# Value projection four heads at a time, and another order of work between the first attention and the expert blocks

## The chip, the cores and the metric

The kernel runs on one core of a Trainium2 chip. The time is device microseconds of one execution; the time before is the median of three runs. The profile is of a further execution of the same program. Engines are named as in the profile: PE (TensorE, with PEld for its weight loads), DVE (VectorE), ACT (ScalarE), POOL (GpSimd), SP (SyncE, which here only issues DMAs).

## The reference

Four sublayers, each `x = x + layernorm(f(layernorm(x)))`, on 2 x 1024 tokens of 128 features in float32. The change touches the first attention and the start of the first feed-forward:

```python
# first attention: 16 heads of 64
qkv = (X @ W_qkv).reshape(b, s, 16, 64, 3); q, k, v = qkv[..., 0], qkv[..., 1], qkv[..., 2]
weights = softmax(einsum('bqhd,bkhd->bhqk', q, k) / 8)
attn = einsum('bhqk,bkhd->bqhd', weights, v); return attn.reshape(b, s, 1024) @ W_out
# first feed-forward: one shared expert and the best 2 of 8 experts, all 128 -> 512 -> 128
normed = hidden * rsqrt(mean(hidden ** 2) + 1e-8) * norm_weight
shared = relu(normed @ sw1 + sb1) @ sw2 + sb2
probs = sigmoid(flat @ router_w.T); scores, idx = top_k(probs, 2)
w = scores / (sum(scores) + 1e-6)     # eo: each expert's output
return shared + sum over the two experts of w * eo
```

The second attention (8 heads, differential) and the gated feed-forward behind it are as before in both kernels.

## The kernel before, in words

Each engine has its own program, written out by hand in order; semaphores tie them together. A value in float32 is held as a rounded part ("hi") and a remainder ("lo"), both in the type fp32r, and a product is two or three matmuls.

**First attention (a0).** 16 heads, one after another. A head has 16 slots, one for each tile of 128 queries (8 tiles of batch 0, then 8 of batch 1). In a slot PE makes the scores (4 matmuls of 512 columns, L643, L644), then perhaps one extra piece, then the 8 transposes of the weights of three slots ago (L611), then 4 matmuls of weights by values (L621, L622). DVE takes the row maximum (L785), its share of the extra piece, and the lo parts of the transposed weights (L771, two of 512). ACT makes exp (L750) and the hi parts (L720). POOL divides by the row sum (L844, L848). The scores have two buffers, the transposed weights two half banks.

The extra pieces are in the table `A0_PIECES`, indexed by the head's place in its pair: `qk` projects queries and keys of a later stretch (3 matmuls of 512), `v` projects values, `out` adds the output projection (8 matmuls of 128). All go through one PSUM bank, `ps_m`: a piece waits until DVE has read the one before (`a0_bank_free`). A `v` piece is 512 tokens by the 128 columns of two heads: per 128 tokens three matmuls of 128 columns (L585 to L587); ACT copies the bank as the hi part (L691), DVE subtracts (L704). `a0_pairs` runs the first pair of heads, a hardware loop of six pairs, and the last pair.

SP places queries and keys with four small DMAs per `qk` piece (`a0_place_qk`), each set behind the previous one. Early in head 0 it also issues the nine loads of the expert weights w1 (`f0_load_early`, 256 KB each), and in head 1 the clearing of the row buffers in DRAM (`f0_clear_rows`).

**Tail and first feed-forward (f0).** The 2048 tokens are 4 chunks of 512. For each, DVE does the norm of the attention's output, adds it to X and norms again in five stages (`y0_norm(stage, chunk)`: 0 statistics of Y, 1 apply, 2 add, 3 statistics of X, 4 apply), with the reciprocal root from POOL (`norm_rstd`, `norm_rstd_rms`). Then PE turns the chunk (`f0_pe_turn`), ACT copies it twice, DVE makes its lo part (`f0_dve_turn`), PE makes router logits (`f0_pe_logits`) and the shared expert (`up`, `down`). For each half of the tokens DVE ranks the experts (`f0_dve_route`: 17 small dependent operations), PE sums prefixes (`route`), DVE works out positions (`f0_dve_place`), and POOL scatters the rows with indirect DMAs (L1475, 16 for a half). Meanwhile w1 is split: ACT copies each of nine pieces as hi (`f0_act_w1_hi`, L982), POOL subtracts (`f0_pool_w1_lo`, L986). When both halves are placed, PE, ACT and DVE read the experts' numbers (`f0_read_words`) and the 46 expert blocks start.

## Time and profile before

| what | value |
|---|---|
| median of 3 runs | 2009.54 us (2009.08 to 2011.68) |
| the profiled execution | 1990.03 us |
| its span, first to last instruction | 1988.2 us |
| granted TensorE clock, mean | 0.971 |
| PE / DVE / ACT / POOL busy | 92% / 78% / 68% / 60% |

The first attention ends at about 875 us, the stretch to the first expert block at about 943 us. A row of the timeline gives start and duration in us, and in brackets how long the engine sat idle before it and what ended that. A matmul's duration is its way through the array; matmuls overlap, so what one costs PE is the distance from its start to the next one's. Where a line groups instructions, the mean is of one.

### The profile page before, as it was taken

The page shows a single profiled execution, that of the slowest core. Times are in us where ns is not written, and L with a number is a line of the kernel's source. Part 1 is how long each engine was busy: PE and PEld are TensorE (multiplying, and loading weights), DVE is VectorE, ACT ScalarE, POOL GpSimd, SP SyncE. Part 2 cuts the span into 40 slices and gives each one's busy share as a digit, 9 for nine tenths or more (in the row PEclk, how much of TensorE's full clock was granted, in tenths as well). Part 3 has the DMA queues.
Part 4 walks back from the last instruction along what each step waited for, and adds up shares of the span by engine and source line. Part 5 has one row for each costly group of instructions (what it writes and reads, how often), then busy time and mean ns, then how long its engine had stood idle before and what let it go on. Part 6 is the DMA issues. An engine that isn't in the chain of part 4 may idle for free.

```text
span 1988.2 us, 37557 instructions
## 1 busy us (share of the span) xinstructions
PE 1838.5 (92%) x11354; PEld 1569.9 (79%) x11354; DVE 1558.7 (78%) x2650; ACT 1351.4 (68%) x2707; POOL 1195.9 (60%) x1481
## 2 busy tenths in 40 slices
PE   4959999999999999985986899999999999999787
PEld 3858888888888888864875688888888888888666
DVE  5958989898989898975577777777777777777775
ACT  3847878787878787841554577777777777777555
POOL 4534646565656465645655577777777777778621
PEclk8979999999999999997998899999999999999899
DMA  4291212121212121112211000000000000100000
GB/s 117 52 82 47 46 40 51 40 51 34 53 35 53 33 55 36 42 49 81 75 58 33 3 1 12 1 11 0 11 0 11 0 11 0 66 1 1 1 11 12
DMA packets 68473, 65.25 MB, mean 33 GB/s; under 512 B 27713, under 2 KB 47041, under 8 KB 68129
## 3 DMA queue, kind: packets, MB, share of 16 engines
q1 hardware_dynamic: 65888, 59.02, 13.7%
q0 software_dynamic: 2496, 5.15, 0.7%
q8 instruction: 44, 0.72, 0.2%
q14 instruction: 45, 0.36, 0.1%
HBM read 21.33 MB, written 9.25 MB: 15 GB/s over the span
## 4 chain that ended last, share of the span: by engine, by line
PE 41%; DVE 7%; issue 4%; ACT 2%; POOL 1%; DVEq 0%; ACTq 0%; POOLq 0%
PE ps_s L1804 5%; PE ps_s L1803 5%; PE ps_s L1805 5%; PE ps_t L1861 3%; PE ps_o L1877 3%; PE ps_o L1879 3%; PE ps_o L1878 3%; PE ps_t L1290 2%; DVE a_negmax L2007 2%; PE ps_m L1898 1%; PE ps_t L1585 1%; PE ps_s L2239 1%; PE ps_s L2240 1%; PE ps_m L1900 1%; PE ps_m L1899 1%
## 5 line engine op out<-in xcount | busy, mean ns | idle before, releaser
L785 DVE TENSOR_REDUCE a_negmax<-ps_s 128x1 f32<-128x1024 f32 x256 | 313.4, 1224 | 73.8 <-PE ps_s L644 59.3
L2007 DVE TENSOR_REDUCE a_negmax<-ps_s 128x1 f32<-128x1024 f32 x256 | 312.3, 1220 | 67.5 <-PE ps_s L1805 64.8
L720 ACT ACTIVATE a_pth<-ps_t 128x512 fp32r<-128x512 f32 x512 | 278.6, 600 | 113.5 <-PE ps_t L611 113.4
L1935 ACT ACTIVATE a_p<-ps_s,a_negmax 128x1024 f32<-128x1024 f32 x256 | 286.4, 1119 | 95.3 <-DVE a_negmax L2007 94.1
L844 POOL TENSOR_TENSOR a_rsum<-a_sum,minus_one 128x1 f32<-128x1 f32 x256 | 141.1, 551 | 329.3 <-ACT a_p L750 328.0
L771 DVE TENSOR_TENSOR a_ptl<-ps_t,a_pth 128x512 fp32r<-128x512 f32 x512 | 327.5, 681 | 6.6 <-ACT a_pth L720 5.8
L848 POOL TENSOR_SCALAR a_p<-a_p,a_rsum 128x1024 f32<-128x1024 f32 x256 | 289.0, 1129 | 52.9 <-POOL a_rsum L844 52.9
L2105 POOL TENSOR_TENSOR a_p<-a_p 128x1024 f32<-128x1024 f32 x128 | 307.4, 2401 | 10.7
L750 ACT ACTIVATE a_p<-ps_s,a_negmax 128x1024 f32<-128x1024 f32 x256 | 288.5, 1127 | 15.3 <-DVE a_negmax L785 15.3
L643 PE MATMUL ps_s<-a_kh,a_q 128*128 128x512 f32 x512 | 202.5, 395 | 30.3 <-DMA a_kl<-a_kl 19.8
L611 PEld LDWEIGHTS ps_t<-ident_r,a_pr 128*128 128x128 f32 x2048 | 200.7, 141 | 31.9 <-POOL a_p L848 4.0
L621 PE MATMUL ps_o<-a_pth,a_v 128*128 128x512 f32 x512 | 220.3, 430 | 3.6 <-ACT a_o L729 2.0
L611 PE MATMUL ps_t<-ident_r,a_pr 128*128 128x128 f32 x2048 | 210.1, 246 | 3.5 <-DVE a_ptl L771 3.5
L1803 PE MATMUL ps_s<-xT_hi,a_q 128*128 128x512 f32 x512 | 203.6, 398 | 7.0 <-ACT a_p L1935 7.0
L1959 ACT ACTIVATE a_ath<-ps_t 128x512 fp32r<-128x512 f32 x256 | 139.2, 596 | 99.2 <-PE ps_t L1861 98.4
L1804 PE MATMUL ps_s<-xT_lo,a_q 128*128 128x512 f32 x512 | 203.0, 397 | 0.0
L1805 PE MATMUL ps_s<-xT_hi,a_q 128*128 128x512 f32 x512 | 202.7, 396 | 0.0
L644 PE MATMUL ps_s<-a_kl,a_q 128*128 128x512 f32 x512 | 202.3, 395 | 0.0
L622 PE MATMUL ps_o<-a_ptl,a_v 128*128 128x512 f32 x512 | 202.0, 395 | 0.0
L2043 DVE TENSOR_TENSOR a_atl<-ps_t,a_ath 128x512 fp32r<-128x512 f32 x256 | 163.6, 680 | 0.5 <-ACT a_ath L1959 0.5
L2099 POOL TENSOR_SCALAR a_p<-a_p,a_c 128x1024 f32<-128x1024 f32 x128 | 144.4, 1128 | 21.9 <-DVE a_c L2020 20.0
L1877 PE MATMUL ps_o<-a_ath,a_xh 128*128 128x256 f32 x512 | 148.2, 289 | 0.6 <-DVE a_atl L2043 0.6
(299 smaller groups left out, 4220.8 us busy)
## 6 DMA issues: line engine op xcount, KB each, us to landing
a_q<-a_kh SPq DMA_DIRECT2D x64, 128.0 KB, 2.2
a_q<-a_kl SPq DMA_DIRECT2D x64, 128.0 KB, 2.4
a_kh<-a_kh SPq DMA_DIRECT2D x64, 128.0 KB, 2.2
a_kl<-a_kl SPq DMA_DIRECT2D x64, 128.0 KB, 2.3
a_w_raw<-in_l_w SPq DMA_DIRECT2D x8, 384.0 KB
f_xs_rows<-f_zero SPq DMA_DIRECT2D x4, 736.0 KB, 20.3
f_raw<-in_ffn_w SPq DMA_DIRECT2D x2, 1408.0 KB, 7.5
f_xs<-f_xs_rows SPq DMA_DIRECT2D x2, 1235.0 KB
```

The lines of the kernel that those rows point to most:

```text
L611: ins = pe.transpose(ps_t[:, half, j * P:(j + 1) * P].bitcast(F32R), a0_pr[q % 4][:, k0:k0 + P], ident_r[:, :])
L720: act.activation(a0_pth[(q // 4) % 2][a0_pt_part(q, half)], ps_t[:, half, :].rearrange("p (t c) -> p t c", c=P), ACT.Copy)\
L750: act.activation(a0_p[s % 4][:, :], ps_s[:, s % 2, :, :], ACT.Exp, bias=a0_negmax[:, s % 4:s % 4 + 1], accum_out=a0_sum[:, s % 4:s % 4 + 1 ...
L771: dve.tensor_tensor(a0_ptl[(q // 4) % 2][at], ps_t[:, half, :].rearrange("p (t c) -> p t c", c=P), a0_pth[(q // 4) % 2][at], ALU.subtract) ...
L785: dve.tensor_reduce(a0_negmax[:, s % 4:s % 4 + 1], ps_s[:, s % 2, :, :], AX.XY, ALU.max, negate=True)\
L848: pool.tensor_scalar(a0_p[s % 4][:, :], a0_p[s % 4][:, :], a0_rsum[:, s % 4:s % 4 + 1], 1.0, ALU.mult, ALU.mult).then_inc(S["a0_p_normed"], 1)
L1803: pe.matmul(dst, a1_q[b][m][:, 0, qs], xT_hi[:, k], start=True, stop=False)
L1804: pe.matmul(dst, a1_q[b][m][:, 0, qs], xT_lo[:, k], start=False, stop=False)
L1805: ins = pe.matmul(dst, a1_q[b][m][:, 1, qs], xT_hi[:, k], start=False, stop=True)
L1935: act.activation(a1_p[s % 4][m][:, :], ps_s[:, m, :, :], ACT.Exp, bias=a1_negmax[:, s % 2, m:m + 1], accum_out=a1_sum[:, s % RING, m:m + 1 ...
L2007: dve.tensor_reduce(a1_negmax[:, s % 2, m:m + 1], ps_s[:, m, :, :], AX.XY, ALU.max, negate=True)\
L2105: pool.tensor_tensor(p1, p1, p2, ALU.add).then_inc(S["a1_combined"], 1)
```

## The change

1. The heads go in fours (`QUAD`, `a0_quads`: first four, a loop of two fours, last four). A `v` piece is now 256 tokens by the 256 columns of four heads: six matmuls of 256 columns in place of twelve of 128. There are eight in the first head of a four and none in the third; each is split by two ACT copies and two DVE subtractions of 256 in place of one each of 512. In all there are 32 `v` pieces before and after.
2. The values' buffer is laid out anew and reaches into the place of w1's raw copy, so w1 is loaded in head 14, when the products of head 13 are done.
3. In the attention's tail: stages of chunk 0's norm go behind the last row maximum; chunk 1's stages 0 to 3 go ahead of DVE's lo part of chunk 0; all nine hi parts of w1 go on ACT ahead of chunk 0's copies, and POOL's nine lo parts follow.
4. Behind the first `up`: chunk 1 is turned and both logits are made, then `down(0)` (with the route's prefix sums inside), `up(1)`, `down(1)`. ACT's relu comes behind the probabilities.

```diff
-            {0: ("out", 1), 1: ("qk", 1, 0), 2: ("v", 0, 0), 3: ("qk", 1, 1), 4: ("out", 2), 5: ("v", 0, 1), 8: ("out", 3),
-             9: ("v", 1, 0), 10: ("qk", 0, 0), 12: ("qk", 0, 1), 13: ("v", 1, 1)},
+            {0: ("out", 1), 1: ("qk", 1, 0), 2: ("v", 0, 0), 3: ("qk", 1, 1), 4: ("out", 2), 5: ("v", 0, 1), 6: ("v", 0, 2),
+             7: ("v", 0, 3), 8: ("out", 3), 9: ("v", 1, 0), 10: ("qk", 0, 0), 11: ("v", 1, 1), 12: ("qk", 0, 1),
+             13: ("v", 1, 2), 14: ("v", 1, 3)},
...
+        def a0_v_of(j, b):
+
+            return a0_v[:, 1 - j // 2, b, :, j % 2, :]
...
+        def a0_quads(eng, body):
+
+            def quad(p, first, last):
+                for j in range(QUAD):
+                    body(p, j, p * QUAD + j, first and j == 0, last and j == QUAD - 1)
+
+            heads(eng, H0 // QUAD, quad)
...
-                for i in range(TPC):
-                    x = slice(b * SEQ + half * BANK + i * P, b * SEQ + half * BANK + (i + 1) * P)
-                    dst = ps_m[:, i * P:(i + 1) * P]
+                for i in range(2):
+                    x = slice(b * SEQ + (2 * half + i) * P, b * SEQ + (2 * half + i + 1) * P)
+                    dst = ps_m[:, i * QUAD * DH0:(i + 1) * QUAD * DH0]
...
-                        if s in (A0_LAG_PV, A0_LAG_PV + KT):
-                            pe.wait_ge(S["a0_split_lo"], a0_splits(p, j, s - 1, last))
+                        if j == 0 and A0_LAG_PV <= s < A0_LAG_PV + 4 or j == 0 and s == A0_LAG_PV + KT:
+                            pe.wait_ge(S["a0_split_lo"], a0_splits(p, j, s - 2, last))
...
-                ins = act.activation(a0_v[b][:, half * TPC:(half + 1) * TPC, :, 0:DH0], src, ACT.Copy)
+                for w in range(2):
+                    ins = act.activation(a0_v[:, w, b, 2 * half:2 * half + 2, :, 0:DH0], src[:, w, :, :, :], ACT.Copy)
...
-                ins = dve.tensor_tensor(v[:, :, :, DH0:2 * DH0], src, v[:, :, :, 0:DH0], ALU.subtract)
+                for w in range(2):
+                    v = a0_v[:, w, b, 2 * half:2 * half + 2, :, :]
+                    ins = dve.tensor_tensor(v[:, :, :, DH0:2 * DH0], src[:, w, :, :, :], v[:, :, :, 0:DH0], ALU.subtract)
...
+            sp.wait_ge(S["a0_pv"], 4 * (H0 - 2))
             for e in range(NE):
                 sp.dma_start(f0_w1_raw[:, e, :], t["ffn0_w1"][:, e, :]).then_inc(S["f0_w1_loaded"], 16)
...
+                    if isinstance(p, int) and p == H0 // QUAD - 1 and j == QUAD - 2 and i == 1:
+                        f0_load_early(sp)
...
             up(0)
+            f0_pe_turn(pe, 1)
             pe.wait_ge(S["a0_out_added"], 2 * H0)
             f0_pe_logits(pe, 0)
-            down(0)
-            f0_pe_turn(pe, 1)
             f0_pe_logits(pe, 1)
+            down(0, lambda: route(0))
             up(1)
-            down(1, lambda: route(0))
+            down(1)
```

**The values on PE.** PE's rows in slot 2 of the first head, from the scores to the next slot's scores. Before (the start of a piece of twelve):

```order
L644 MATMUL ps_s<-a0_kl0,a0_q0 128x512
L585 MATMUL ps_m<-a0_wv_hi,xT_hi 128x128 [waits a0_wv_lo,a0_split_lo]
L586 MATMUL ps_m<-a0_wv_lo,xT_hi 128x128
L587 MATMUL ps_m<-a0_wv_hi,xT_lo 128x128
L585 MATMUL ps_m<-a0_wv_hi,xT_hi 128x128
L586 MATMUL ps_m<-a0_wv_lo,xT_hi 128x128
L587 MATMUL ps_m<-a0_wv_hi,xT_lo 128x128
L585 MATMUL ps_m<-a0_wv_hi,xT_hi 128x128
```

After, the whole piece:

```order
L658 MATMUL ps_s<-a0_kl0,a0_q0 128x512
L599 MATMUL ps_m<-a0_wv_hi,xT_hi 128x256 [waits a0_wv_lo,a0_split_lo]
L600 MATMUL ps_m<-a0_wv_lo,xT_hi 128x256
L601 MATMUL ps_m<-a0_wv_hi,xT_lo 128x256
L599 MATMUL ps_m<-a0_wv_hi,xT_hi 128x256
L600 MATMUL ps_m<-a0_wv_lo,xT_hi 128x256
L601 MATMUL ps_m<-a0_wv_hi,xT_lo 128x256
L657 MATMUL ps_s<-a0_kh0,a0_q0 128x512 [waits a0_exped]
```

Twelve matmuls of 128 columns became six of 256.

**The norms on DVE.** DVE's rows around the last row maximum of the attention (`f0_staged0` is chunk 0's norm, `ptl` the lo parts). Before:

```order
L785 TENSOR_REDUCE a0_negmax<-ps_s 128x1 [waits a0_scores]
L771 TENSOR_TENSOR a0_ptl0<-ps_t,a0_pth0 128x4x128 [waits a0_pt_hi] x2
L371 TENSOR_SCALAR f0_staged0<-Y,mv,rstd 128x128 [waits norm_rstd]
L371 TENSOR_SCALAR f0_staged0<-Y,mv,rstd 128x128 x3
L785 TENSOR_REDUCE a0_negmax<-ps_s 128x1 [waits a0_scores]
L771 TENSOR_TENSOR a0_ptl1<-ps_t,a0_pth1 128x4x128 [waits a0_pt_hi] x2
L943 TENSOR_TENSOR X<-X,f0_staged0 128x512 [waits dve_step]
```

After:

```order
L807 TENSOR_REDUCE a0_negmax<-ps_s 128x1 [waits a0_scores]
L793 TENSOR_TENSOR a0_ptl0<-ps_t,a0_pth0 128x4x128 [waits a0_pt_hi] x2
L807 TENSOR_REDUCE a0_negmax<-ps_s 128x1 [waits a0_scores]
L793 TENSOR_TENSOR a0_ptl1<-ps_t,a0_pth1 128x4x128 [waits a0_pt_hi] x2
L373 TENSOR_SCALAR f0_staged0<-Y,mv,rstd 128x128 [waits norm_rstd]
L373 TENSOR_SCALAR f0_staged0<-Y,mv,rstd 128x128 x3
L793 TENSOR_TENSOR a0_ptl1<-ps_t,a0_pth1 128x4x128 [waits a0_pt_hi] x2
L976 TENSOR_TENSOR X<-X,f0_staged0 128x512 [waits dve_step]
```

The last row maximum and the lo part behind it passed the four apply operations.

**The tail on ACT.** ACT's rows from the first hi part of w1 on (`a0_o2` are the attention's last outputs, `f0_nT`, `xT_hi` the turned chunk, `f0_h` the shared expert's relu). Before:

```order
L729 ACTIVATE a0_o20<-ps_o 128x512 [waits a0_out_in,a0_pv]
L967 ACTIVATE f0_nT0<-ps_t,f0_nw 128x512 [waits f0_logits,x_turned,f0_small_loaded]
L460 ACTIVATE xT_hi<-ps_t,f0_nw 128x512 [waits x_turned]
L729 ACTIVATE a0_o21<-ps_o 128x512 [waits a0_out_in,a0_pv]
L982 ACTIVATE f0_w1_hi<-f0_w1_raw 128x512 [waits f0_w1_loaded]
L1335 ACTIVATE f0_h00<-ps_s,f0_b1 128x512 [waits f0_up]
```

After:

```order
L747 ACTIVATE a0_o20<-ps_o 128x512 [waits a0_out_in,a0_pv]
L1015 ACTIVATE f0_w1_hi<-f0_w1_raw 128x512 [waits f0_w1_loaded] x6
L747 ACTIVATE a0_o21<-ps_o 128x512 [waits a0_out_in,a0_pv]
L1000 ACTIVATE f0_nT0<-ps_t,f0_nw 128x512 [waits f0_logits,x_turned,f0_small_loaded]
L462 ACTIVATE xT_hi<-ps_t,f0_nw 128x512 [waits x_turned]
L1000 ACTIVATE f0_nT1<-ps_t,f0_nw 128x512 [waits f0_logits,x_turned]
L462 ACTIVATE xT_hi<-ps_t,f0_nw 128x512 [waits x_turned]
L1034 ACTIVATE f0_prob<-ps_m 128x64 [waits f0_logits]
L1368 ACTIVATE f0_h00<-ps_s,f0_b1 128x512 [waits f0_up]
```

Six hi parts stand between the last two outputs, and the first relu stands behind chunk 1's copies and the probabilities.

## Rows read from the trace of the kernel before

**Rows 1.** The page: busy time and share of the span, by engine.
```profile
PE 1838.5 (92%) x11354; PEld 1569.9 (79%) x11354; DVE 1558.7 (78%) x2650; ACT 1351.4 (68%) x2707; POOL 1195.9 (60%) x1481
```
**Rows 2.** Windows: stretch, its length, busy of each engine, PEclk, DMA share, GB/s.
```profile
460.00:560.00 100.00, 99.64 (x640) 85.83 (x640) 87.82 (x112) 79.20 (x147) 55.78 (x71) 1.00 0.18 43
```
**Rows 3.** Timeline of PE: a v piece's first matmul, and what follows its twelfth.
```profile
256.86 0.23 PE L585 MATMUL ps_m<-a_wv_hi,xT_hi 128*128 128x128 f32 x1
...
258.15 0.85 PE L611 MATMUL ps_t<-ident_r,a_pr 128*128 128x128 f32 x8
```
**Rows 4.** Timeline of PE: twelve matmuls of 256 columns in the second attention.
```profile
1302.05 0.28 PE L1877 MATMUL ps_o<-a_ath,a_xh 128*128 128x256 f32 x1
...
1303.47 0.39 PE L1803 MATMUL ps_s<-xT_hi,a_q 128*128 128x512 f32 x1
```
**Rows 5.** Timeline of DVE: row maxima that begin a qk, a plain and a v slot.
```profile
205.94 1.23 DVE L785 TENSOR_REDUCE a_negmax<-ps_s 128x1 f32<-128x1024 f32 x1
...
209.20 1.22 DVE L785 TENSOR_REDUCE a_negmax<-ps_s 128x1 f32<-128x1024 f32 x1
...
220.09 1.22 DVE L785 TENSOR_REDUCE a_negmax<-ps_s 128x1 f32<-128x1024 f32 x1
...
222.64 1.23 DVE L785 TENSOR_REDUCE a_negmax<-ps_s 128x1 f32<-128x1024 f32 x1
...
257.06 1.23 DVE L785 TENSOR_REDUCE a_negmax<-ps_s 128x1 f32<-128x1024 f32 x1
...
260.94 1.23 DVE L785 TENSOR_REDUCE a_negmax<-ps_s 128x1 f32<-128x1024 f32 x1
```
**Rows 6.** Lines by form: copies and subtractions from PSUM of 512 and of 256.
```profile
L691 ACT ACTIVATE a_v<-ps_m 128x512 fp32r<-128x512 f32 x32 | 19.2, 599 | 40.1 <-PE ps_m L587 40.1
L1968 ACT ACTIVATE a_zh<-ps_o 128x256 fp32r<-128x256 f32 x64 | 24.0, 375 | 2.1 <-PE ps_o L1879 2.1
L704 DVE TENSOR_TENSOR a_v<-ps_m,a_v 128x512 fp32r<-128x512 f32 x32 | 22.1, 692 | 22.1 <-ACT a_v L691 22.0
L2049 DVE TENSOR_TENSOR a_zl<-ps_o,a_zh 128x256 fp32r<-128x256 f32 x3 | 1.3, 422 | 1.8 <-ACT a_zh L1968 1.8
```
**Rows 7.** Timeline: PE's wait in the attention's tail, first up, chunk 1's turn.
```profile
855.75 1.25 PE L611 MATMUL ps_t<-ident_r,a_pr 128*128 128x128 f32 x8 [1.86 <-DVE a_ptl L771]
...
875.41 0.48 PE L1232 MATMUL ps_s<-xT_hi,f_w_hi 128*128 128x512 f32 x1
...
882.91 0.60 PE L454 MATMUL ps_t<-ident,f_staged 128*128 128x128 f32 x4
```
**Rows 8.** Timeline: POOL's lo parts of w1 over DVE's first route, one same operation later.
```profile
887.43 8.66 POOL L986 TENSOR_TENSOR f_w_lo<-f_w_raw,f_w_hi 128x512 fp32r<-128x512 f32 x7
...
891.32 1.19 DVE L1020 TENSOR_TENSOR f_tmp<-f_tmp,f_rank 128x64 f32<-128x64 f32 x1
...
899.86 0.17 DVE L1061 CAST f_pos<-f_place 128x16 int32<-128x16 f32 x1
...
928.03 0.22 DVE L1020 TENSOR_TENSOR f_tmp<-f_tmp,f_rank 128x64 f32<-128x64 f32 x1
```
**Rows 9.** Timeline of PE: chunk 2's turn, and the first turn of the expert blocks.
```profile
908.62 1.11 PE L454 MATMUL ps_o<-ident,f_staged 128*128 128x128 f32 x4 [7.70 <-DVE f_staged L371]
...
936.67 0.50 PE L1262 MATMUL ps_o<-ident_r,f_xs 128*128 128x128 f32 x4 [4.09 <-issue]
```
**Rows 10.** Timeline: four apply operations of DVE, undisturbed and while POOL works.
```profile
876.30 1.11 DVE L371 TENSOR_SCALAR f_staged<-Y,mv,rstd 128x128 f32<-128x128 f32 x4
...
1106.79 3.96 DVE L371 TENSOR_SCALAR xhat<-Y,mv,rstd 128x128 f32<-128x128 f32 x4
...
1108.21 2.46 POOL L2105 TENSOR_TENSOR a_p<-a_p 128x1024 f32<-128x1024 f32 x1
```
**Rows 11.** Timeline: PE's wait in head 2; DMA view: w1's loads, KB each, us to landing.
```profile
145.34 0.79 PE L643 MATMUL ps_s<-a_kh,a_q 128*128 128x512 f32 x1 [19.76 <-DMA a_kl<-a_kl]
...
f_w_raw<-in_ffn_w SPq DMA_DIRECT2D x9, 256.0 KB, 4.5
```

More of the change, by code:

```diff
@@ L80, in sandwich_kernel @@
         A0_END = 137 * KB
+        QUAD = 4
         A1_KEYS = 109 * KB
@@ L538, in sandwich_kernel, with a0_pair @@
         A0_SPLITS = [[s for s in pieces if pieces[s][0] != "out"] for pieces in A0_PIECES]
-        A0_PAIR_SPLITS = len(A0_SPLITS[0]) + len(A0_SPLITS[1])
+        A0_QUAD_SPLITS = sum(len(z) for z in A0_SPLITS)
+        def a0_pair(p, j):
+            return p * 2 + j // 2
         def a0_piece(j, s, first, last):
             piece = A0_PIECES[j].get(s)
-            if piece is None or (first and piece[0] == "out" and j == 0) or (last and j == 1 and s in A0_NEXT):
+            if piece is None or (first and piece[0] == "out" and j == 0) or (last and j == QUAD - 1 and s in A0_NEXT):
                 return None
@@ L548, in a0_splits @@
         def a0_splits(p, j, s, last):
-            n = sum(1 for z in A0_SPLITS[j] if z <= s and not (last and j == 1 and z in A0_NEXT))
-            return p * A0_PAIR_SPLITS + (len(A0_NEXT) + j * len(A0_SPLITS[0]) + n)
+            n = sum(1 for z in A0_SPLITS[j] if z <= s and not (last and j == QUAD - 1 and z in A0_NEXT))
+            return p * A0_QUAD_SPLITS + (len(A0_NEXT) + sum(len(z) for z in A0_SPLITS[:j]) + n)
         def a0_outs(p, j, s):
-            return p * 4 + (3 * j - 3 + sum(1 for z in A0_PIECES[j] if z <= s and A0_PIECES[j][z][0] == "out"))
+            return a0_pair(p, j) * 4 + (3 * (j % 2) - 3 + sum(1 for z in A0_PIECES[j] if z <= s and A0_PIECES[j][z][0] == "out"))
         def a0_bank_free(pe, p, j, s, first, last):
@@ L565, in a0_bank_free @@
                 pe.wait_ge(S["a0_split_lo"], a0_splits(p, j, z, last))
-        def a0_pairs(eng, body):
-            def pair(p, first, last):
-                for j in range(2):
-                    body(p, j, p * 2 + j, first and j == 0, last and j == 1)
-            heads(eng, H0 // 2, pair)
+        def a0_quads(eng, body):
[3 more added lines that the diff above has]
+            heads(eng, H0 // QUAD, quad)
         def first_bank(i):
@@ L907, in body @@
                     sp.dma_start(a0_wqk_raw[:, :], row(t["l0_wqk"], h + 1)).then_inc(S["a0_wqk_loaded"], 16)
-                if j == 1 and not last:
+                if j == QUAD - 1 and not last:
                     sp.wait_ge(S["a0_wv_lo"], p + 1)
```

120 lines of the change are left out of this document (63 added, 57 removed), and 3 rows, old and new, of the table A0_PIECES.

## The prediction

> **What bounds the kernel now.** I read the busy shares first, then windows, then timelines of the two places that the change touches. PE is busy for 92% of the span [rows 1]. In the steady part of the first attention it is busy for 99.64 of 100 us at the full granted clock, DVE for 87.82, ACT for 79.20, POOL for 55.78 [rows 2]: PE sets the pace there and every us taken from its queue counts, as long as DVE, the next one, stays below it. It is close in a plain slot: the row maxima of two plain slots stand 2.55 us apart (222.64 - 220.09), and DVE needs one maximum and two lo parts in it. A `qk` slot takes 3.26 us and a `v` slot 3.88 [rows 5]. Behind the attention nobody is full. From 875 to 943 us the time goes along a chain: chunk 1's norm, turn and logits, the route on DVE, positions, chunk 2's norm between POOL's scatters, its turn on PE at 908.62 after 7.70 us of idling, and at the end the reading of the experts' numbers before PE turns the first expert rows at 936.67 [rows 9].
>
> **The values, four heads a pass.** Twelve matmuls of 128 columns take PE from 256.86 to 258.15, 1.29 us or 0.108 each; a `v` slot is longer than a plain one by 3.88 - 2.55 = 1.33 us [rows 3, 5]. Twelve matmuls of 256 columns in the second attention go from 1302.05 to 1303.47, 1.42 us or 0.118 each, again in fp32r with a new weight tile for each [rows 4]. So a matmul of half the columns costs nearly as much, and six of 256 cost 6 x 0.118 = 0.71 us where twelve of 128 cost 1.29 to 1.33. There are 32 pieces before and 32 after. Saved on PE: 32 x 0.60 = 19.2 us.
>
> The Trainium skill (TensorE: Matmul & The Clock Gate, "Back-to-back issue gap") gives, for a matmul alone, 134 cycles for 128 columns and 262 for 256. By that twelve small ones cost what six large ones cost, and the merge gives nothing; the trace has 0.108 us for 128 columns, about twice that rule, and 0.118 for 256, so it disagrees for the small one, and I follow the trace. It stays a rival below.
>
> Against it stands the split. ACT's copy of 512 takes 599 ns, of 256 375, so two take 750: 0.15 us more. DVE's subtraction takes 692 and 422, two 844: 0.15 us more [rows 6]. They lie beside PE as long as DVE keeps up. A `qk` slot, built the same way, costs 3.26 - 2.55 = 0.71 us over a plain one [rows 5]; a `v` slot should be the same if DVE and ACT hide their part, and 0.30 more if neither does: 3.26 to 3.56 us, against 3.88. Ends: 32 x 0.60 = 19.2 and 32 x 0.32 = 10.2. I take 18.5, near the upper end, since the slots of 4 heads average out: only the first head of four holds `v` pieces, its `out` slots leave DVE idle, and DVE has 12 us of slack in 100 [rows 2]. The bank `ps_m` is now used in 15 of 16 slots there; before, slots 0 to 5 already followed each other without a PE wait.
>
> Waits added. PE's waits for `a0_split_lo` ask for pieces of two slots ago, which the bank's own wait has already asked for: 0. SP now waits in head 14 for the products of head 13 (slot 6) before the w1 loads, and behind it in its queue stand the two last placements of head 14, from slot 10 on, some 10 us later. Each load landed 4.5 us after its issue at the start of the kernel [rows 11]; if the nine hardly overlapped they would take 9 x 1 us and more, still within those 10, and head 15 needs the placements only at its start, nine slots of at least 2.55 us after slot 6: hidden. Taking the loads away from head 0 gains nothing: PE's 19.76 us wait in head 2 [rows 11] comes behind the clearing of the rows, which stays. Two more small value loads stand ahead of three of the X loads: +0.5 us, between 0 and 1. The loop is entered half as often; no wait stands at its branches, so 0.
>
> **The tail.** (a) The last row maximum no longer waits for the four apply operations, so the 1.86 us that PE waits at 855.75 go [rows 7]: -1.9. (b) POOL's seven lo parts of w1 lie over DVE's route, 887.43 to 896.09, and seven of its two-input operations take 0.94 to 1.21 us each in place of about 0.22 (1.19 against 0.22 for the same line later) [rows 8]: 7.7 us in place of 1.6. With w1 split ahead of it: -6.1. (c) Chunk 1's turn comes at 882.91, 7.5 us behind the start of the first `up` [rows 7], after logits, `down(0)` and a norm that started late. After the change the norm's stages 0 to 3 run while PE does the last output pieces, and the turn follows `up` at once: `up` is twelve matmuls of twice the columns of rows 4, 2 x 1.42 = 2.8 us, so up to 7.5 - 2.8 = 4.7 us are saved; and the first `up` itself starts 2 to 3 us sooner, since nothing of chunk 0 waits behind the last output: -7 together if nothing interferes. (d) Something does: POOL's nine lo parts now lie over chunk 0's last apply and chunk 1's stages 1, 2 and 4, ten DVE operations on SBUF. Rows of before show what happens to them: four apply operations that take 1.11 us undisturbed took 3.96 with POOL at work, ending with its 2.46 us operation [rows 10]. At one lo part each (8.66 / 7 = 1.24 us [rows 8]) in place of 0.26 the ten lose up to 9.8 us, partly in waits that are there anyway: +5, between 0 and 9.8. (e) PE idles for the relus, which now stand behind the probabilities, before `down(0)`: four of about the 0.6 us of rows 6, near 3 us with the handover; but the route runs beside it and is the longer way, and `up(1)`, `down(1)` end about when chunk 2 is ready for its turn: 0 to +3.
>
> The positions of the first half, at 899.86 [rows 8], come sooner by 1.9 + 6.1 + 7 - 5 = 10; all behind them (scatters, chunk 2's norm, its turn, the second route, the expert numbers) is a chain that keeps its length, so the first turn of the blocks at 936.67 [rows 9] moves by as much, less (e). I take -9.5 for the tail. Ends: 1.9 + 6.1 + 7 = 15, and 15 - 9.8 - 3 = 2.
>
> The Trainium skill (SBUF — State Buffer, "Who interferes with whom") says that DVE operations with two SBUF inputs and those in two-port modes, `tensor_scalar` among them, are held off entirely while GpSimd works, and the other way round. Rows 8 and 10 agree. By it term (d) is real, and (b) is only moved, not removed, in so far as the norms are on the chain too.
>
> **Sum.** -18.5 + 0.5 - 9.5 = -27.5 us. The sum is made against the profiled execution, 1990.03 us: 1962.5. The median of the runs stands 19.5 us above it, about the same program; I carry the difference over unchanged: 2009.5 - 27.5 = 1982.
>
> **The rivals.**
> - The merge gives nothing (the width, not the count, is what PE pays; this is where the page's rule leads). For it: PE streams twice the columns in each matmul. Against it: rows 3 and 4 side by side. Then only the tail counts: 2009.5 - 9 = 2000.5.
> - The port of DVE and POOL eats the whole tail: term (d) at its full 9.8, PE idling while it waits. Tail 0 or little: 2009.5 - 18 = 1991.
> - The w1 loads hold up head 15. Row clearing did that to head 2 (19.76 us [rows 11]). For it: nine loads of 256 KB stand before a placement. Against it: they landed in 4.5 us each at the start, and there are some 10 us before the next placement and 9 x 2.55 = 23 before head 15. Price up to 20: 2001.
> - Slower: the one bank. PE's piece, two ACT copies, two DVE subtractions and PE's next piece form a ring through `ps_m` in 15 successive slots. If the ring, and not PE, sets the slot, each of the 32 `v` slots takes longer; the merge's gain is gone when such a slot costs 3.88 us, and with the tail's 9.5 the kernel is slower when it costs over 3.88 + 9.5/32 = 4.2. Summed from the rows the ring is 0.71 + 0.75 + 0.84 and three handovers of about 0.25, 3.1 us and below the slot, so this needs handovers of 0.6. At 4.4 us: 32 x 0.5 - 9.5 = +7, 2016.
>
> **How the numbers follow.** Forecast (both gains, 1971 to 1990): 0.72. Tail eaten: 0.12. Merge without gain: 0.05. Loads in the way: 0.05. The one bank, slower: 0.03. The rest, 0.03, ends near no change. Best case by the terms: 19.2 + 15 = 34 gives 1975, and I allow 4 us more for waits of PE that go with its shorter queue; worst of the terms: 10.2 + 2 - 1 = 11 gives 1998. The range of 8 in 10 is 1971 to 1995. What a measurement of this kernel can tell from no change is about 0.2%, 4 us. Faster by more: 0.95; within: 0.02; slower: 0.03.
>
> **What would show it.** In the profile after, six matmuls of 256 columns take 0.7 us between scores and transposes, and row maxima of `v` slots stand 3.3 us apart; 3.5 or more says that DVE or ACT sets them. The distance from head to head: the third of four shorter by some 5 us, the first about as before. PE idle at L643's counterpart only at the start and once after row clearing; a wait at head 15 speaks for the loads. DVE's route under 5.5 us; apply operations of 1 us and more beside POOL's lo parts show (d). First turn of expert rows some 28 us sooner than 936.67. The prediction is wrong if the attention ends less than 10 us sooner, or if the stretch from its end to the blocks is not shorter.

## The result, and the profile after

| kernel | median of its runs, us | the profiled execution | its span |
|---|---|---|---|
| before, beside the changed kernel | 2009.31 (2008.22 to 2011.68, 4 runs) | 1990.03 | 1988.2 |
| changed | 1987.55 (1985.73 to 1988.88, 4 runs) | 1987.63 | 1985.6 |

The ratio is 0.989, 95% interval 0.9872 to 0.9907: 21.8 us or 1.1% faster. Forecast were 1982 and a range of 1971 to 1995. The two traces, though, are only 2.6 us apart. The 19.5 us that stood between the first profile and the timed runs of the kernel before go with the chip in every group of experiments below. So each pair compared here comes from chips of the same kind: rows of before with a second profile of the changed kernel (span 1964.9), and a second profile of the kernel before (2005.8) with the changed kernel's first (1985.6).

| from, to | before | changed, second profile | difference | before, second profile | changed | difference |
|---|---|---|---|---|---|---|
| start to last row maximum of the first attention | 853.79 | 833.10 | -20.7 | 848.33 | 833.31 | -15.0 |
| to first `up` | 21.62 | 26.26 | +4.6 | 23.88 | 26.28 | +2.4 |
| to first scatter | 24.93 | 15.42 | -9.5 | 25.08 | 15.44 | -9.6 |
| to first turn of expert rows | 36.33 | 33.68 | -2.7 | 41.59 | 42.47 | +0.9 |
| to first row maximum of the second attention | 121.46 | 121.10 | -0.4 | 134.80 | 135.09 | +0.3 |
| to its last | 797.60 | 800.48 | +2.9 | 799.38 | 798.68 | -0.7 |
| to the end | 132.5 | 134.9 | +2.4 | 132.8 | 134.3 | +1.5 |
| sum | 1988.2 | 1964.9 | -23.3 | 2005.8 | 1985.6 | -20.2 |

Two things are mixed into the first line. The wait behind the row clearing [rows 11], which the change leaves alone, is 19.8 us in the first profile, then 17.1, 14.3 and 16.5 from left to right. And the change moves the last row maximum itself: the last head takes 42.3 us from its first row maximum to its last, before 44.2, so 1.9 us of what the tail wins stand in this line.

The page of the changed kernel, busy time and share by engine, and its two queues of instruction packets (packets, MB, share), to be read beside [rows 1]:

```profile
PE 1826.1 (92%) x11162; PEld 1557.8 (78%) x11162; DVE 1556.2 (78%) x2682; ACT 1354.5 (68%) x2739; POOL 1196.3 (60%) x1473
...
q8 instruction: 71, 1.16, 0.3%
q14 instruction: 76, 0.62, 0.1%
```

PE has 192 matmuls fewer (32 pieces by 6). The same window of the steady attention as [rows 2]:

```profile
460.00:560.00 100.00, 99.68 (x640) 86.24 (x639) 90.41 (x123) 81.45 (x158) 55.52 (x70) 1.00 0.20 46
```

PE is still the bound (99.68); DVE has risen from 87.82 to 90.41. A `v` piece on PE, beside [rows 3]; the last row is the transposes behind it:

```profile
259.83 0.28 PE L599 MATMUL ps_m<-a_wv_hi,xT_hi 128*128 128x256 f32 x1
...
260.43 0.28 PE L601 MATMUL ps_m<-a_wv_hi,xT_lo 128*128 128x256 f32 x1
260.55 0.80 PE L625 MATMUL ps_t<-ident_r,a_pr 128*128 128x128 f32 x8
```

0.72 us for the piece (0.71 forecast): from its first matmul to the transposes. Each matmul has a weight load of its own, though not always a new tile (L599 and L600 load the same one); the page has as many loads as matmuls, 11162. DVE's slot of that piece, beside [rows 5]:

```profile
260.03 1.23 DVE L807 TENSOR_REDUCE a_negmax<-ps_s 128x1 f32<-128x1024 f32 x1 [0.36 <-PE ps_s L658]
261.44 0.76 DVE L722 TENSOR_TENSOR a_v<-ps_m,a_v 128x256 fp32r<-128x256 f32 x2 [0.19 <-ACT a_v L708]
262.12 1.28 DVE L793 TENSOR_TENSOR a_ptl<-ps_t,a_pth 128x512 fp32r<-128x512 f32 x2
263.31 1.22 DVE L807 TENSOR_REDUCE a_negmax<-ps_s 128x1 f32<-128x1024 f32 x1
```

The slot is 3.28 us, the lower end of the forecast 3.26 to 3.56. The two subtractions together take 0.76 us; the 0.84 of the prediction is twice the mean of one, and here they overlap. DVE has 0.19 us of idling left in it, so this slot is close to DVE's bound as well.

PE's waits between 60 and 833 us (us in total, times, longest):

```profile
PE ps_s L657 <- DMA a_kh<-a_kh: 16.5, 1, 16.5
PE ps_s L657 <- issue: 3.6, 1, 3.6
```

The first is the wait behind the row clearing [rows 11]. The second is new. It stands where the loop of fours jumps back:

```profile
441.07 0.79 PE L657 MATMUL ps_s<-a_kh,a_q 128*128 128x512 f32 x1 [3.57 <-issue]
```

The DMA view of 436 to 442 us shows eight packets of instructions in those 6 us:

```profile
q8 instruction: 2, 0.03, 3.1%
q14 instruction: 6, 0.05, 2.4%
```

The wait is not all that the jump costs. Behind it PE runs at half its clock for a while; the granted clock is the third number from the end of each row:

```profile
437.40:440.50 3.10, 0.10 (x1) 0.00 (x0) 0.73 (x2) 0.85 (x2) 1.21 (x3) 1.00 0.03 11
441.10:443.90 2.80, 2.80 (x9) 2.42 (x10) 0.72 (x1) 0.00 (x0) 0.22 (x1) 0.50 0.03 6
```

DVE's row maxima that begin the last head ahead of the jump and the second head behind it:

```profile
392.39 1.23 DVE L807 TENSOR_REDUCE a_negmax<-ps_s 128x1 f32<-128x1024 f32 x1 [0.32 <-PE ps_s L658]
498.67 1.23 DVE L807 TENSOR_REDUCE a_negmax<-ps_s 128x1 f32<-128x1024 f32 x1 [0.44 <-PE ps_s L658]
```

These two heads take 106.3 us. The same two places of a four with no jump between them, from 594.40 to 695.51, take 101.1. So the jump costs 5.2 us: 3.6 of waiting, and some 1.6 at the low clock behind it.

The tail, beside [rows 7, 10]. DVE, POOL and PE in order of time:

```profile
841.66 4.97 POOL L1019 TENSOR_TENSOR f_w_lo<-f_w_raw,f_w_hi 128x512 fp32r<-128x512 f32 x4
```
```profile
841.77 4.95 DVE L373 TENSOR_SCALAR f_staged<-X,mv,rstd 128x128 f32<-128x128 f32 x4
846.64 1.28 DVE L793 TENSOR_TENSOR a_ptl<-ps_t,a_pth 128x512 fp32r<-128x512 f32 x2
```
```profile
847.97 0.80 PE L635 MATMUL ps_o<-a_pth,a_v 128*128 128x512 f32 x1 [4.52 <-DVE a_ptl L793]
```

Four apply operations keep step with POOL's four lo parts, 1.24 us each, and a lo part of the attention's weights, which PE waits for, stands behind them. Again the low clock comes on top: from the end of that wait on, 5.4 us of PE's work run at half the clock.

```profile
848.00:853.40 5.40, 5.40 (x17) 4.63 (x18) 1.08 (x8) 0.00 (x0) 3.78 (x5) 0.50 0.01 3
```

The first turn of expert rows, beside [rows 9], in the second profile of the changed kernel:

```profile
908.46 0.72 PE L1295 MATMUL ps_o<-ident_r,f_xs 128*128 128x128 f32 x4 [4.10 <-issue]
```

It comes 28.2 us sooner than 936.67. Of these 28.2 us 2.7 are luck: the row-clearing wait, untouched by the change, happened to be that much shorter in this trace.

### The profile page after: what moved, and what is told of

It is laid out like the page before. It is cut to its first block, busy times and chain, and to the rows that moved or that the text cites. A ratio compares the mean times of both kernels' runs of the same rounds, so it can differ in the third digit from the quotient of the medians.

```text
span 1985.6 us, 36444 instructions
## 1 busy us (share of the span) xinstructions
PE 1826.1 (92%) x11162; PEld 1557.8 (78%) x11162; DVE 1556.2 (78%) x2682; ACT 1354.5 (68%) x2739; POOL 1196.3 (60%) x1473
## 4 chain that ended last, share of the span: by engine, by line
PE 77%; DVE 9%; issue 5%; ACT 4%; SPq 2%; POOL 2%; DMA 1%; another core or an unknown queue 1%; DVEq 0%; ACTq 0%; POOLq 0%
PE ps_t L625 7%; PE ps_o L635 6%; PE ps_s L657 5%; PE ps_s L658 5%; PE ps_o L636 5%; PE ps_s L1831 5%; PE ps_s L1829 5%; PE ps_s L1830 5%; PE ps_t L1887 3%; PE ps_o L1903 3%; PE ps_o L1905 3%; PE ps_o L1904 3%; PE ps_t L1323 2%; DVE a_negmax L2033 1%; PE ps_m L614 1%
## 5 line engine op out<-in xcount | busy, mean ns | idle before, releaser
L2125 POOL TENSOR_SCALAR a_p<-a_p,a_c 128x1024 f32<-128x1024 f32 x128 | 144.5, 1129 | 22.3 <-DVE a_c L2046 19.9
```

## The experiments

Two theories and a question stood at the start. By the terms of the prediction the merge wins 18.5 us and the tail 9.5. By the first two traces the tail wins nothing, since the first turn of the expert rows in the changed kernel's first profile comes only 19.2 us sooner, hardly more than the end of the attention. The question was what the 19.5 us are. Kernels that stand in one group below ran on one chip, beside the kernel before.

**First group: the halves of the change.** Before: 2007.46 (17 runs).

`e1_merge_only`: the change without its parts 3 and 4.

```diff
             f0_act_w1_hi(act, 0)
-            f0_act_w1_hi(act, 1)
             pt_hi(g - 2, SLOTS - 2)
-            f0_act_w1_hi(act, 2)
             pt_hi(g - 1, SLOTS - 1)
...
             up(0)
-            f0_pe_turn(pe, 1)
             pe.wait_ge(S["a0_out_added"], 2 * H0)
             f0_pe_logits(pe, 0)
+            down(0)
+            f0_pe_turn(pe, 1)
             f0_pe_logits(pe, 1)
```

> The changed kernel with the old tail: heads in fours, values of four heads in one pass, the new place of the values' buffer and the late w1 loads, but the norms, w1's split, turns, logits and relus in the old order. Terms theory (the merge gives 18.5 us, the tail 9.5): 2009.3 - 18 = 1991. Rival from the two traces: the tail gives nothing at the end, since in the trace of the changed kernel the first turn of the expert rows comes 19.2 us sooner, no more than the end of the attention does (20.5); then this kernel runs like the changed one, 1987.5. Second rival: the time that the kernel before spends outside its profile (19.5 us) goes with the merge alone, then also 1985 to 1990, but its attention would still end some 20 us sooner in the profile.

Measured: 1991.69 (1989.24 to 1999.23), ratio 0.993 (0.9908 to 0.9951): 15.8 us faster. Its page has the same instruction packets as the changed kernel's (71 and 76), and its attention has the new wait:

```profile
PE ps_s L657 <- DMA a_kh<-a_kh: 15.8, 1, 15.8
PE ps_s L657 <- issue: 3.3, 1, 3.3
```

The two heads around the jump take 106.3 us here too. With the row-clearing wait taken off, the attention's last row maximum stands at 819.8 (835.60 - 15.8), where both profiles of the kernel before have 834.0: 14.2 us.

`e2_tail_only`: parts 3 and 4 on the kernel before, the values' buffer moved off the norms' place.

```diff
-        sb(None, A0_END)
+        sb(None, A0_END - B * KT * 4 * DH0 * 4 - 2 * 2 * DH0 * 4)
+
+        a0_wv_hi = sb("a0_wv_hi", [P, 2 * DH0], F32R)
+        a0_wv_lo = sb("a0_wv_lo", [P, 2 * DH0], F32R)
+        a0_v = [sb(f"a0_v{b}", [P, KT, 2, 2 * DH0], F32R) for b in range(B)]
...
             up(0)
+            f0_pe_turn(pe, 1)
             pe.wait_ge(S["a0_out_added"], 2 * H0)
             f0_pe_logits(pe, 0)
-            down(0)
-            f0_pe_turn(pe, 1)
             f0_pe_logits(pe, 1)
+            down(0, lambda: route(0))
```

> The kernel before with the new tail only: heads in pairs, twelve matmuls of 128 columns for a piece of values, w1 loaded at the start; the norms, w1's split, turns, logits and relus in the new order (the values' buffer is only moved to where nothing of the tail lies). Terms theory: 2009.3 - 9.5 = 2000. Rival (the tail's gain is lost to waits behind POOL's lo parts and in the first expert blocks): 2009, no change. In the profile the stretch from the last row maximum to the first turn of expert rows tells: before 936.67 less 853.8 is 82.9 us; terms theory 73, rival 82 to 84.

Measured: 2000.94 (1997.96 to 2002.91), ratio 0.9967 (0.9955 to 0.9979): 6.5 us faster. From the last row maximum (847.94) to the first turn of expert rows (930.67) it takes 82.7 us; `e1_merge_only`, with the old tail and on the same chip, has 87.7, and to the 5.0 between them come the 1.9 by which the maximum itself is moved. (The second profile of before, on another chip, has 90.6; the 82.9 in the expectation are of the other kind of chip.) No wait `<- issue` in its attention; 44 and 45 instruction packets, as before. The halves add: 15.8 + 6.5 = 22.3, and the whole gives 21.8. The tail wins something, so the second theory falls.

`e3_narrow`: PE's twelve matmuls of 128 columns in the changed kernel.

```diff
-                    dst = ps_m[:, i * QUAD * DH0:(i + 1) * QUAD * DH0]
-                    pe.matmul(dst, xT_hi[:, x], a0_wv_hi[:, :], start=True, stop=False)
+                    for w in range(2):
+                        c = slice(w * 2 * DH0, (w + 1) * 2 * DH0)
+                        dst = ps_m[:, i * QUAD * DH0 + w * 2 * DH0:i * QUAD * DH0 + (w + 1) * 2 * DH0]
+                        pe.matmul(dst, xT_hi[:, x], a0_wv_hi[:, c], start=True, stop=False)
...
```

> The changed kernel, but each piece of values is issued as twelve matmuls of 128 columns in place of six of 256: same data, same splits, only PE's count of matmuls differs. Price per matmul (0.108 us at 128 columns against 0.118 at 256): 32 pieces x 0.6 = 19 us slower than the changed kernel, 1987.5 + 19 = 2006. Rival (PE pays by the column): the same time as the changed kernel, 1987.5. Second rival (the slot of a piece of values is set by DVE and the bank, 3.27 us, and PE has room in it): between, 5 to 12 us slower.

Measured: 2005.25 (1999.39 to 2006.65), ratio 0.9987 (0.9977 to 0.9997). Against the changed kernel's ratio 0.989 that is 1.0% or 19 us slower. DVE's row maxima that begin three `v` slots:

```profile
261.67 1.22 DVE L809 TENSOR_REDUCE a_negmax<-ps_s 128x1 f32<-128x1024 f32 x1 [0.35 <-PE ps_s L660]
...
265.58 1.23 DVE L809 TENSOR_REDUCE a_negmax<-ps_s 128x1 f32<-128x1024 f32 x1
...
269.47 1.23 DVE L809 TENSOR_REDUCE a_negmax<-ps_s 128x1 f32<-128x1024 f32 x1
```

3.90 us a slot against 3.28, with the same splits: the count of matmuls alone costs 0.62 us a piece. The figures for a matmul alone that the prediction took from the Trainium skill (TensorE: Matmul & The Clock Gate, "Back-to-back issue gap"), 134 cycles for 128 columns and 262 for 256, would have had no difference here; the runs disagree. The same section also has about 81 ns for a matmul of 128 columns in a stream with weight loads, which the prediction left out; the 108 ns of [rows 3] are above that too.

`e4_clear_spread`: the six clearing DMAs two each in heads 1, 2 and 3.

```diff
-                    if isinstance(p, int) and p == 0 and j == 1 and i == 1:
-                        f0_clear_rows(sp)
+                    if isinstance(p, int) and p == 0 and j > 0 and i == 1:
+                        f0_clear_rows(sp, (2 * j - 2, 2 * j - 1))
```

> The changed kernel, but the six DMAs that clear the row buffers are set two each in heads 1, 2 and 3, between the placements of slots 3 and 10, in place of all six in head 1. If PE's wait of 16.50 us at 143.22 comes only from SP's queue (placements stand behind the six, some 7 us each): the wait goes, 1987.5 - 16 = 1971. Rival: the clearing DMAs fill the DMA engines, placements take longer in three heads and each stalls a little: 1980 to 1988.

Measured: 1968.63 (1966.22 to 1973.08), ratio 0.9815 (0.9795 to 0.9836), 0.75% or some 15 us below the changed kernel's. The attention's last row maximum comes at 814.72 in place of 833.31, 18.6 us sooner, 2 more than the wait of 16.5; behind that wait, too, the changed kernel's granted clock is 0.5 until 146.9 us, and here it is not. PE's waits between 60 and 833 us no longer have the DMA (the first one here is the tail's, which now falls into this window):

```profile
PE ps_o L635 <- DVE a_ptl L793: 4.5, 1, 4.5
PE ps_s L657 <- issue: 3.4, 1, 3.4
```

**Second group: a second profile, and two terms of the tail.** Before: 2008.94 (13 runs).

`e5_before_again`: no edit.

> The kernel before, unchanged, profiled once more. Its first profiled execution took 1990.03 us, its 21 timed runs 2004 to 2012; the changed kernel's profiled execution takes what its timed runs take. Theory that the first profile was an unusually quick execution: this one takes 2004 to 2012 us, and its trace shows PE held up where the four profiles of the variants show it (a wait of some 3.2 us for f_pre in the tenth expert block, 4 to 6 us of idling before the last router logits), together 15 to 20 us that the first profile lacks. Rival (the profiler itself changes this kernel's pace): again 1990 us and no such waits.

Measured: 2009.46 (2003.93 to 2012.7), span 2005.8. So the profiler does not change the pace, and the first profile was the exception. What the first profile lacks is between the first turn of the expert rows and the sixteenth block, and ahead of the last logits:

```profile
PE ps_s L1282 <- DVE f_pre L1399: 4.5, 3, 1.9
PE ps_t L1290 <- ACT f_bh L1351: 4.3, 4, 2.0
PE ps_t L1290 <- issue: 1.6, 1, 1.6
```

These are PE's waits from 945 to 1031 us; in the first profile the same stretch shows none for `f_bh`. The changed kernel's first profile has such a place most plainly. DVE, then ACT, then PE (`remote` is a semaphore whose rise the profile gives to no instruction):

```profile
944.50 0.69 DVE L1426 COPY f_pre<-ps_s 128x512 f32<-128x512 f32 x1 [0.25 <-PE ps_s L1307]
951.50 0.29 DVE L1433 TENSOR_TENSOR f_ys<-ps_t,f_b 128x128 f32<-128x128 f32 x1 [6.31 <-remote]
```
```profile
945.74 1.15 ACT L1384 ACTIVATE f_bh<-ps_s,f_b 128x128 f32<-128x128 f32 x4 [2.23 <-PE ps_s L1315]
951.51 1.15 ACT L1384 ACTIVATE f_bh<-ps_s,f_b 128x128 f32<-128x128 f32 x4 [4.62 <-remote]
```
```profile
946.25 0.45 PE L1315 MATMUL ps_s<-ident_r,f_prer 128*128 128x128 f32 x4
947.01 1.13 PE L1323 MATMUL ps_t<-f_w,f_bh 128*128 x8 [0.31 <-ACT f_bh L1384]
...
948.81 0.40 PE L1307 MATMUL ps_s<-f_w_hi,f_xs_lo 128*128 x1
952.45 0.74 PE L1315 MATMUL ps_s<-ident_r,f_prer 128*128 128x128 f32 x4 [3.24 <-DVE f_pre L1426]
```

DVE and ACT both wait for a semaphore of PE's whose matmul the trace has at 945.45; in the trace's semaphore events it rises at 951.22, and five more rises of PE's semaphores, of matmuls that the trace has from 946.02 to 948.81, follow by 951.53. Work that the trace spreads over 3 us and that is signalled within 0.3 speaks for matmuls that had run and whose signals were held up; this is argued from the times, no run shows it apart. The Trainium skill (Perfetto Trace Analysis, "Summary: the profiler window per engine type") says that TensorE's end is estimated in the trace; that agrees with rows of PE that show nothing of the delay.

`e6_lo_parts_back`: POOL's nine lo parts of w1 in the old places.

```diff
-            for pos in range(4):
-                f0_pool_w1_lo(pool, pos)
+            f0_pool_w1_lo(pool, 0)
             norm_rstd(pool, norm_a0(1, 0), 1)
+            f0_pool_w1_lo(pool, 1)
...
             norm_rstd(pool, norm_a0(3, 0), 3)
+            for pos in range(2, NE):
+                f0_pool_w1_lo(pool, pos)
```

> The changed kernel, but POOL's nine lo parts of w1 stand where they stood before: one behind the first norm, one behind the second, seven behind the norms of chunks 2 and 3. Terms theory: PE's wait of 4.52 us for the lo part of the weights at 847.97 goes (5 us won, term d), and the route is slowed by POOL's seven operations again (6.1 us lost, term b): 1 us slower, 1988.6, and the route on DVE takes 5 us more than in the changed kernel. Rival (the norms do not matter, the route is the chain): 5 to 6 us slower, 1993. Second rival (the route does not mind): 4 us faster, 1983.5.

Measured: 1987.26 (1985.06 to 1989.51), ratio 0.9888 (0.9868 to 0.9908): the same as the changed kernel's. From the last row maximum to the first `up` 20.3 us in place of 26.3 (term d: 6.0), from there to the first scatter 19.7 in place of 15.4 (term b: 4.3). The 6.0 have two halves. PE's wait for the lo part of the weights is 1.60 us and not 4.52, and the granted clock stays at 1.00 behind it:

```profile
844.82 0.50 PE L635 MATMUL ps_o<-a_pth,a_v 128*128 128x512 f32 x1 [1.60 <-DVE a_ptl L793]
```
```profile
843.30:848.00 4.70, 3.19 (x20) 2.86 (x21) 2.62 (x12) 3.67 (x7) 1.54 (x3) 1.00 0.02 3
```

From the end of that wait to the first product behind the output pieces PE needs 3.63 us (844.82 to 848.45), in the changed kernel 6.22 (847.97 to 854.19). So 2.9 us of the 6.0 are the longer wait and 2.6 the low clock behind it. POOL's operations are over the route again:

```profile
859.70 8.59 POOL L1019 TENSOR_TENSOR f_w_lo<-f_w_raw,f_w_hi 128x512 fp32r<-128x512 f32 x7
873.08 1.27 POOL L1500 DMA_INDIRECT f_xs_rows<-f_staged,f_pos  x1 [4.79 <-DVE f_pos L1094]
```

From DVE's first operation on the probabilities (L1048) to the marks of the chosen experts (L1059) the route takes 9.5 us here and 3.6 in the changed kernel, 5.9 less, but there DVE then waits 1.0 for PE's prefix sums. So the two prices nearly cancel: 1.7 us are left in the traces at the first scatter, which the timed runs, 0.3 us apart, can't tell from nothing.

`e7_relu_first`: ACT's first relus ahead of chunk 1's turn.

```diff
+            relu(0)
             f0_act_turn(act, 1)
             f0_act_probs(act, 0)
-            relu(0)
```

> The changed kernel, but ACT does the first relus before the copies of chunk 1's turn and the probabilities, as in the kernel before. Terms theory (e): PE's 2.63 us wait before down(0) at 868.05 goes, but the probabilities come some 2.8 us later (four relus of 0.6 to 0.7) and with them the route, positions and scatters: 2 to 3 us slower, 1990. Rival (PE's wait was on the path): 2 us faster, 1985.

Measured: 1985.02 (1983.63 to 1986.75), ratio 0.9876 (0.9858 to 0.9893), on the better side of the changed kernel's, but the intervals overlap. In its trace first `up` to first scatter is 14.3 us, not 15.4. The relus delay nothing:

```profile
859.51 2.78 ACT L1368 ACTIVATE f_h<-ps_s,f_b 128x512 f32<-128x512 f32 x4 [2.31 <-PE ps_s L1267]
862.50 0.69 ACT L1000 ACTIVATE f_nT<-ps_t,f_nw 128x512 f32<-128x512 f32 x1 [0.21 <-PE ps_t L456]
```

In the changed kernel ACT idles there until chunk 1's turn:

```profile
863.56 0.69 ACT L1000 ACTIVATE f_nT<-ps_t,f_nw 128x512 f32<-128x512 f32 x1 [5.49 <-PE ps_t L456]
```

The turn is later than the scores of `up`, so the relus find room. My expectation was wrong: it had the relus in front of the turn's copies, and they are, but in time that was idle.

**Third group: a chip of the other kind.** Before: 1991.04 (7 runs).

`e8_after_again`: no edit.

> The changed kernel, unchanged, on the same chip as the next two, to compare them with. 1985 to 1990 us; its profile with PE's completions late in the first expert blocks, as in the changed kernel's first profile and in the second profile of the kernel before.

Measured: 1966.72 (1965.97 to 1969.69), ratio 0.9886 (0.9862 to 0.9909). The time is 21 us below the expectation, the ratio the same as at first. In its trace no semaphore of PE's rises over 1.5 us behind the record of its matmul. In the changed kernel's first trace 31 do, in the second profile of before 35, in its first one 1 (where the trace lacks a rise, the next one of that semaphore is taken). The waits of PE from 915 to 1000 us, all of them:

```profile
PE ps_s L1305 <- DVE f_xs_lo L1418: 6.1, 2, 5.7
PE ps_s L1315 <- DVE f_pre L1426: 3.3, 3, 1.5
PE ps_s L1305 <- issue: 0.2, 1, 0.2
```

With it the 19.5 us have a place: on two chips (this one and that of `e12`) the kernel before takes 1987 to 1991, on two others 2007 to 2009, where PE's signals are held up. All traces divide in the same way. In eight there are 28 to 35 late rises, and from the first turn of expert rows to the second attention it takes 133.0 to 135.1 us; in the other six there are 0 to 2, and it takes 120.9 to 121.5. The first profile of before is one of the six, its timed runs took what the eight take. Each chip was measured at one time only, and the two quick ones last, so that the chip itself is the reason is likely and not shown.

`e9_scatter_ahead` and, on a fourth chip, `e12_scatter_ahead_2`: the second half's 16 indirect DMAs ahead of the blocks.

```diff
-            for i in range(2):
+            for i in range(GT):
                 scatter(1, i)
             for n in range(BLOCKS):
-                if n % 2 == 0 and 2 + n // 2 < GT:
-                    scatter(1, 2 + n // 2)
                 send(n)
```

> The changed kernel, but POOL issues all 16 indirect DMAs of the second half's rows ahead of the first block's, in place of 4 ahead and 12 between the first blocks' results. Theory that PE's completions are held while POOL's indirect DMAs follow each other without a pause (in the changed kernel's trace they come in a burst at 940.4, 951.2, 959.3 and 967.3, each time when that queue's traffic stops): with the sends alone POOL has pauses from the ninth block on, and some of the 13 us are won: 1977 to 1983. Rival (the holds have nothing to do with it): same time, 1987.5. Second rival (the first sends, 15 us later, hold DVE up through the ring of eight buffers): 1990 or more.

> The kernel of the scatter-ahead run again. On a chip that holds PE's completions back, theory of pauses: 1977 to 1983 where the changed kernel takes 1987.5, and fewer late completions between the first block and the sixteenth than the 13 us that the changed kernel loses there. Rival: 1987 and the same 13 us. On a chip that does not: the same as its first run, some 1967.9.

Measured: 1967.85 (1964.61 to 1968.61), ratio 0.9889 (0.9867 to 0.9911); and 1966.41 (1965.67 to 1969.03), ratio 0.9894 (0.9873 to 0.9915). No change against the changed kernel. But both chips were of the kind that holds nothing up, so the theory that POOL's indirect DMAs hold the signals up while they follow each other without a pause wasn't put to the test: inconclusive.

`e10_three_edits` is e4, e6 and e7 together; `e11_four_edits` adds that of e9.

> The changed kernel with three edits together: the clearing DMAs spread over heads 1 to 3, POOL's lo parts of w1 back in their old places, the first relus ahead of chunk 1's turn. If they add up: 1968.6 (spread alone) less 2.5 (relus) less 0.3 (lo parts) = 1966. Rival (the lo parts' place and the relus' work on the same stretch and do not add): 1968 to 1970.

> The changed kernel with the three edits of before (clearing spread, POOL's lo parts back, relus first) and the second half's 16 indirect DMAs ahead of the first block's. On a chip that does not hold PE's completions back nothing is won by the fourth edit: the ratio to the kernel before stays at 0.979. On one that does, the theory of pauses on POOL says 4 to 10 us less: ratio 0.974 to 0.977; the rival says 0.981, where the changed kernel's 0.989 and the spread's 0.9815 lie.

Measured: 1948.77 (1947.31 to 1950.11), ratio 0.9794 (0.9772 to 0.9816), 18.0 us below `e8_after_again` on the same chip, of which the wait of 17.1 us behind the row clearing there is nearly all; and 1948.66 (1946.45 to 1949.06), ratio 0.98 (0.9782 to 0.9817). Both beat both kernels. The expected 1966 was for the other kind of chip; the sum of the three edits, 21 to 22 us, was too much by 3 or 4.

## Why the prediction was right, by its steps

**The merge (-18.5).** Right in mechanism, and 2.7 us too small for the pieces alone. PE's price of a piece fell from 1.29 to 0.72, the `v` slot from 3.88 to 3.28 [rows 5 for before's slots]; four heads without the jump take 196.7 us (195.67 to 392.39), before 202.1, which for 16 heads makes 21.2 us, and `e3_narrow` puts it on the count of matmuls. As forecast the third head of four is the shorter one, 49.7 us where before had 55.0. That DVE and ACT hide the doubled split was right, but only just: DVE is left 0.19 us in such a slot. The ring through one bank, the slower rival, did not come near its 4.2 us. The rival that the width is what PE pays is refuted. The prediction's words "with a new weight tile for each" are wrong in this, that each matmul loads its weights, the same tile now and then; the sum doesn't change by it.

**"The loop is entered half as often; no wait stands at its branches, so 0"** is the step that failed. The jump costs 5.2 us: PE waits 3.57 us at 441.07 for nothing that the profile shows, and runs at the low clock behind that. The kernel before fetched no instructions from 445 to 745 us; the body of four heads is twice as long, and in that stretch 16 and 17 packets are fetched, with a burst at the jump. `e1_merge_only` has the wait (3.3), `e2_tail_only` not, so it belongs to the heads in fours; that it is the fetch that PE waits for is argued from the packets. The net of the merge is 21.2 - 5.2 = 16.0, and 15.8 were timed. The sign that the prediction named, PE idle only at the start and behind the row clearing, failed by the same wait.

**w1 loads, `a0_split_lo` waits, start (+0.5).** Right: no wait at head 15, none for the added semaphores; the first head takes 46.6 us, before 45.5 or 45.8. The row clearing's wait stays, as said, but its size varies from one execution to the next: 14.3 to 19.8 us over eleven traces that have it. In one pair of the table it fell by 2.7, in the other it rose by 2.2; that is 4.9 of the 5.7 us between the two differences of the first line.

**The tail (-9.5).** Right in sign, too large by 3: 6.5 were timed alone. (The tables have -7.6 and -6.3 up to the first turn, and 1.9 for the maximum that was moved, but they compare different chips: the second profile of before needs 2.3 us longer to the first `up` than the first one.) Its parts: (b) -6.1 is right for the route itself (-5.9) and 4.3 at the scatter. (d) +5 was 6.0, by `e6`, but only 2.9 of them are the wait for DVE that the term is made of; 2.6 are the low clock behind it, which the prediction doesn't have. Of the two costs of POOL and DVE side by side one was swapped for the other. The Trainium skill (SBUF — State Buffer, "Who interferes with whom") was right about both kinds of DVE operation that it has blocked while GpSimd works, `tensor_scalar` and those with two inputs in SBUF: the four applies take 4.95 us beside POOL, and the seven route operations 7.4 us in `e6`, 1.6 without POOL. (a) -1.9: right, the last head is 1.9 shorter. (c) The forecast that the first `up` starts 2 to 3 us sooner failed: it is 4.6 and 2.4 us later, counted from the last row maximum, all by (d). In `e6`, without (d), it is 1.3 sooner, and 3.2 with the maximum's own 1.9. What was won behind it, 9.5 us to the first scatter, is (b) and the earlier turn of chunk 1. (e) 0 to +3 was about 1, and it had another reason than I gave: with the relus first, ACT's idle time takes them.

**"All behind them is a chain that keeps its length".** Nearly. The change has chunk 3's reciprocal root one scatter earlier (`if i == 2`), which I passed over: 2 indirect DMAs at 1.27 us, and the stretch from scatter to first turn is 2.7 us shorter in one pair. How much of it is won depends on the granted clock there: the other four traces with the root in this place and without held signals take 35.3 to 37.6 us for the stretch, not 33.7; in the one with 37.6 the granted clock is 0.80 from 877 to 897 us, in the one with 33.7 it is 1.00 from 880 to 900. In the other pair it is swallowed by the held signals ahead of the last logits, where PE waits 7.1 us and before 4.2. Blocks: unchanged within 0.4.

**What I did not foresee** are 5.3 us behind the blocks in the one pair and 0.8 in the other. In the first, the second attention and the rest have a lower granted clock: 0.98 and 0.89 against 0.99 and 0.90 (before, then changed):

```profile
1058.10:1855.70 797.60, 764.57 (x4682) 654.35 (x4681) 628.23 (x1102) 554.86 (x1162) 584.99 (x666) 0.99 0.03 9
1855.70:1988.20 132.50, 106.05 (x466) 84.80 (x466) 85.59 (x222) 71.08 (x116) 41.03 (x58) 0.90 0.03 9
```
```profile
1029.60:1830.00 800.40, 768.21 (x4682) 659.24 (x4680) 628.64 (x1102) 554.85 (x1162) 583.68 (x666) 0.98 0.03 9
1830.00:1964.90 134.90, 108.79 (x466) 87.07 (x466) 85.66 (x222) 71.42 (x116) 41.03 (x58) 0.89 0.03 8
```

PE has the same matmuls and 3.6 + 2.7 us more of busy time. Why the clock was lower here was not tested.

**Carrying the 19.5 us over** came out right, but the prediction gave no reason for it: the changed kernel was timed where the runs of the kernel before take 2009 us too, and on the chip of the third group, where it takes 1966.7, the forecast of 1982 would have been off by 15. Measured were 21.8 us and not 27.5. By the halves timed alone 2.2 of the missing us are the merge's (15.8 for 18.0, the pieces' extra gain less the jump) and 3.0 the tail's (6.5 for 9.5).

## What to carry to other kernels

Matmuls of 128 columns with a weight load each cost PE nearly what those of 256 do (0.108 and 0.118 us here): double the columns where a bank and the next engine allow it, and read that engine's idling in the new slot, which is what is left to win. Unrolling a loop's body further is not free: look for instruction packets in the DMA view and for a wait `<- issue` at the jump. Price an idle stretch of PE with the low clock behind it: here 3.6 us of waiting cost 5.2. Before a tail is reordered around two engines that hold each other up, as DVE and POOL do here, price both places: 4.3 us were won and 6.0 lost, while one DMA queue's order, untouched by the change, held 17 us.
